# A short form for the last group of an expert, when it holds at most 128 rows

## The reference

```python
probs = softmax(x @ gate_w); w, sel = top_k(probs, 8); w = w / sum(w)     # 32 experts
# each expert takes its rows in order of token, at most C = 2048 of them
xg = x_pad[t_slot].reshape(E, C, H)
g = einsum('ech,ehi->eci', xg, w_gate)      # 512 -> 192
u = einsum('ech,ehi->eci', xg, w_up)        # 512 -> 192
y = einsum('eci,eih->ech', silu(g) * u, w_down).reshape(E * C, H)
out = zeros((T + 1, H)).at[t_slot].add(w_slot[:, None] * y)
```

## Time and profile before

| | |
|---|---|
| median of 3 runs | 2157.45 us (2155.42 to 2159.64) |
| span of the profiled execution | 2155.5 us |
| expert phase in it | about 1096 to 2145 us |
| PE busy | 1944.1 us, 90% |
| DVE busy | 1582.7 us, 73% |
| ACT busy | 1203.0 us, 56% |
| POOL busy | 1575.2 us, 73% |

### The profile page before, as it was taken

One profiled execution on the slowest core, in us unless ns is written; L12 is line 12 of the kernel. 1 busy time (PEld: TensorE's weight loads), 2 busy tenths in 40 slices (PEclk: granted clock), 3 DMA queues, 4 the chain that ended last, 5 costly groups with the idle time before them and its releaser, 6 DMA issues. The chain is left out here.

```text
span 2155.5 us, 66447 instructions
## 1 busy us (share of the span) xinstructions
PE 1944.1 (90%) x22263; PEld 1463.4 (68%) x22296; DVE 1582.7 (73%) x3230; ACT 1203.0 (56%) x3018; POOL 1575.2 (73%) x1776
## 2 busy tenths in 40 slices
PE   0799999999999999997259999999999999999997
PEld 0677667777667766675146777777777777777775
DVE  5688888888888888985236676777766667767664
ACT  3466666666666666665135555555554555545553
POOL 6336778777777777876667777777767777777775
PEclk9999999999999999999579999999999999999999
DMA  3111110111101111101048888777788888887876
GB/s 108 38 34 37 40 39 30 34 34 40 39 29 34 34 39 39 32 27 43 16 111 172 186 193 160 176 181 171 167 178 186 170 178 182 169 190 156 184 153 103
DMA packets 141452, 222.72 MB, mean 103 GB/s; under 512 B 32944, under 2 KB 65840, under 8 KB 141360
## 3 DMA queue, kind: packets, MB, share of 16 engines
q0 software_dynamic: 74752, 144.02, 33.9%
q1 hardware_dynamic: 62000, 69.24, 10.4%
q10 hardware_dynamic: 4608, 8.39, 1.0%
HBM read 136.34 MB, written 96.73 MB: 108 GB/s over the span
## 5 line engine op out<-in xcount | busy, mean ns | idle before, releaser
L2162 POOL DMA_INDIRECT out_dram<-y,m_add x300 | 498.1, 1660 | 171.0 <-POOLq L2170 112.5
L2288 PE MATMUL ps<-xh,wh 128*128 128x256 f16 x1752 | 398.3, 273 | 4.7 <-PEq L2300 4.7
L2289 PE MATMUL ps<-xh,wl 128*128 128x256 f16 x1752 | 398.3, 273 | 0.0
L2154 POOL DMA_INDIRECT xg<-z_scratch,slot_t x292 | 295.8, 1013 | 96.4 <-issue 83.4
L630 POOL DMA_INDIRECT slot_scratch<-pair,slots x256 | 304.8, 1191 | 70.2 <-issue 58.1
L2365 ACT ACTIVATE y<-ps,wts_now 128x512 f32<-128x512 f32 x294 | 185.2, 681 | 143.4 <-ACTq L2364 143.4
L2293 PE MATMUL ps<-xl,wh 128*128 128x256 f16 x1752 | 239.0, 273 | 1.3 <-PEq L2304 1.3
L2439 DVE SCALAR_TENSOR_TENSOR hx<-ps,s 64x256 f16<-64x256 f32 x146 | 62.2, 426 | 216.3 <-DVEq L2462 215.6
L2381 ACT ACTIVATE xh<-ps 128x512 f16<-128x512 f32 x146 | 87.2, 597 | 224.0 <-ACTq L2380 224.0
L2288 PEld LDWEIGHTS ps<-xh,wh 128*128 128x128 f16 x1752 | 171.3, 98 | 45.9 <-issue 12.8
L2289 PEld LDWEIGHTS ps<-xh,wl 128*128 128x128 f16 x1752 | 171.4, 98 | 33.1
(11 more groups left out here) (345 smaller groups left out, 5001.4 us busy)
## 6 DMA issues: line engine op xcount, KB each, us to landing
wst<-in_L_ffn_w_gate_dram SPq DMA_DIRECT2D x32, 384.0 KB
wst<-in_L_ffn_w_up_dram SPq DMA_DIRECT2D x32, 384.0 KB
xt<-in_x_dram SPq DMA_DIRECT2D x32, 256.0 KB
ct<-in_ctx_dram SPq DMA_DIRECT2D x32, 256.0 KB, 2.6
out_dram<-x SPq DMA_DIRECT2D x32, 256.0 KB, 2.1
z_scratch<-zn ACTq DMA_DIRECT2D x32, 256.0 KB, 2.0
wdst<-in_L_ffn_w_down_dram SPq DMA_DIRECT2D x32, 256.0 KB
out_dram<-y,m_add POOLq DMA_INDIRECT x300, 5.1
```

What stands on the lines that cost most here:

```text
L2154: pool.indirect_dma_start(out=xg[b][:, h, :], out_offset=None, in_=z_d[:, :], in_offset=bass.IndirectOffsetOnAxis(ap=rows(h), axis=0)).the ...
L2162: pool.indirect_dma_start(out=acc_d[:, :], out_offset=bass.IndirectOffsetOnAxis(ap=m_add[:, k, h:h + 1], axis=0), in_=y[:, k, h, :], in_of ...
L2288: pe.matmul(ps[:, dst, 0:GROUP], wh[:, j, k, c0:c0 + P], xh[:, k, :], start=(k == 0), stop=False)
L2289: pe.matmul(ps[:, dst, 0:GROUP], wl[:, j, k, c0:c0 + P], xh[:, k, :], start=False, stop=False)
```

## The change

A last group of an expert with at most 128 rows gets a form of its own on PE, if it is group 2, 3 or 4. (`ends_short(n)` is true for 513 to 640, 769 to 896 and 1025 to 1152 rows.) Of the 32 experts 16 meet this: 0, 7, 9 and 10 with four groups and 2, 6, 11, 12, 18, 20, 23, 24, 25, 28, 29 and 30 with five.

In that form POOL gathers one half of 128 rows into a buffer `xs` of its own, after it has copied the 128 row numbers with an operation of its own; PE transposes 4 times instead of 8 and runs `gate_up` with 128 columns instead of 256. `down`, ACT and DVE do what they did, over all 256 columns (the second half holds old values, whose rows are not added to the output). The form stands once for each place of an expert in the program, behind groups 2 to 4 and the further ones. The further groups now all run in one small loop.

```diff
-            def written_out_groups(eng, n, group):
+            def written_out_groups(eng, n, group, least=1):
                 for g in range(2, USUAL):
-                    with eng.If(n > g * GROUP):
+                    with eng.If(n >= g * GROUP + least):
                         group(g, g)
                 with eng.If(n > USUAL * GROUP):
-                    group(USUAL, 2)
-                    with eng.Fori(USUAL + 1, NGRP) as g:
+                    with eng.Fori(USUAL, NGRP) as g:
                         with eng.If(n > g * GROUP):
-                            group(g, 3)
+                            group(g, 2)
+            def ends_short(n):
+                halves = (n - 1) // P
+                return (halves // 4) * ((16 - halves) // 8) * (1 - halves % 2) > 0
...
+                def gather_short(e, n):
+                    col = e * (CAP // P) + 2 * ((n - 1) // GROUP)
+                    pool.wait_ge(short_free, 1)
+                    pool.sem_inc(short_free, -1)
+                    pool.tensor_copy(short_rows[:, :], slot_t[:, bass.ds(col, 1), 0]).then_inc(short_rows_ready, 1)
+                    pool.wait_ge(short_rows_ready, 1)
+                    pool.sem_inc(short_rows_ready, -1)
+                    pool.indirect_dma_start(out=xs[:, :], out_offset=None, in_=z_d[:, :],
+                                            in_offset=bass.IndirectOffsetOnAxis(ap=short_rows[:, 0:1], axis=0)).then_inc(short_landed, 16)
...
-                    with pool.If(n > 2 * GROUP):
+                    with pool.If(n > 2 * GROUP + P):
                         gather_group(e, 2, 2)
                     add_rows(y_buffer(0))
-                    with pool.If(n > 3 * GROUP):
+                    with pool.If(n > 3 * GROUP + P):
                         gather_group(e, 3, 3)
+                    with pool.If(ends_short(n)):
+                        gather_short(e, n)
                     earlier_experts_added()
...
-                        with pool.If(n > 4 * GROUP):
+                        with pool.If(n > 4 * GROUP + P):
                             gather_group(e, 4, 4)
...
+                def turn_short():
+                    pe.reg_add(n_short, n_short, 16)
+                    pe.wait_ge(short_landed, pe.snap(n_short, min_val=16, max_val=16 * E))
+                    for bank, signal in ((0, rows_ps_act), (1, rows_ps_dve)):
+                        for n in range(2):
+                            k = 2 * bank + n
+                            m = pe.transpose(ps[:, bank, n * GROUP:n * GROUP + P], xs[:, k * P:(k + 1) * P], ident[:, :])
+                        m.then_inc(signal, 1)
...
-                            pe.matmul(ps[:, dst, 0:GROUP], wh[:, j, k, c0:c0 + P], xh[:, k, :], start=(k == 0), stop=False)
+                            pe.matmul(ps[:, dst, 0:cols], wh[:, j, k, c0:c0 + P], xh[:, k, 0:cols], start=(k == 0), stop=False)
...
                     group(1, 1)
                     n = count_of(pe, e)
-                    written_out_groups(pe, n, group)
+                    written_out_groups(pe, n, group, P + 1)
+                    with pe.If(ends_short(n)):
+                        turn_short()
+                        down(j, short_free)
+                        gate_up(j, P)
```

More of the change, by code:

```diff
@@ L2075, in build @@
             y = sb("y", [P, YBUF, 2, D])
+            xs = sb("xs", [P, D])
+            short_rows = sb("short_rows", [P, 1], U32)
+            short_landed = sem("short_landed")
+            short_free = sem("short_free")
+            short_rows_ready = sem("short_rows_ready")
             w_staged = sem("w_staged")
@@ L2208, in expert @@
                             gather_group(e + 1, 1, 1)
-                        with pool.If(n > 4 * GROUP):
+                        with pool.Else():
                             gather_group(e + 1, 0, 0)
@@ L2222, in expert @@
                         with pool.If(n > g * GROUP):
-                            gather_group(e, g, 3)
+                            gather_group(e, g, 2)
                             add_rows(y_buffer(g))
@@ L2227, in _ @@
                     pool.sem_inc(rows_free[b], 1)
+                pool.sem_inc(short_free, 1)
                 pool.wait_ge(slots_loaded, 16)
@@ L2249, in _ @@
                     pe.reg_mov(n_landed[b], 0)
+                n_short = pe.alloc_register("n_short")
+                pe.reg_mov(n_short, 0)
                 def turn(b):
@@ L2260, in turn, with down @@
                         m.then_inc(signal, 1)
-                def down(j, b=None):
+                def turn_short():
[6 more added lines that the diff above has]
+                        m.then_inc(signal, 1)
+                def down(j, free=None):
                     pe.wait_ge(hx2_ready, 2)
@@ L2268, in down @@
                         m = pe.matmul(o, hx2[:, t], dh[:, j, 1, :], start=True, stop=False)
-                        if h == 0 and b is not None:
-                            m.then_inc(rows_free[b], 1)
+                        if h == 0 and free is not None:
+                            m.then_inc(free, 1)
                         pe.matmul(o, hx2[:, t], dl[:, j, 1, :], start=False, stop=False)
@@ L2282, in down, with gate_up @@
                         pe.matmul(o, hl1[:, t], dh[:, j, 0, :], start=False, stop=True).then_inc(y_ps, 1)
-                def gate_up(j):
+                def gate_up(j, cols=GROUP):
                     def with_xh(c0, dst):
                         for k in range(KC):
-                            pe.matmul(ps[:, dst, 0:GROUP], wh[:, j, k, c0:c0 + P], xh[:, k, :], start=(k == 0), stop=False)
-                            pe.matmul(ps[:, dst, 0:GROUP], wl[:, j, k, c0:c0 + P], xh[:, k, :], start=False, stop=False)
+                            pe.matmul(ps[:, dst, 0:cols], wh[:, j, k, c0:c0 + P], xh[:, k, 0:cols], start=(k == 0), stop=False)
+                            pe.matmul(ps[:, dst, 0:cols], wl[:, j, k, c0:c0 + P], xh[:, k, 0:cols], start=False, stop=False)
                     def with_xl(c0, dst, signal):
                         for k in range(KC):
-                            m = pe.matmul(ps[:, dst, 0:GROUP], wh[:, j, k, c0:c0 + P], xl[:, k, :], start=False,
+                            m = pe.matmul(ps[:, dst, 0:cols], wh[:, j, k, c0:c0 + P], xl[:, k, 0:cols], start=False,
                                           stop=(k == KC - 1))
@@ L2311, in expert @@
                     turn(0)
-                    down(1 - j, 0)
+                    down(1 - j, rows_free[0])
                     pe.wait_ge(wh_ready[j], 1)
@@ L2318, in group @@
                         turn(b)
-                        down(j, b)
+                        down(j, rows_free[b])
                         gate_up(j)
```

## The result

The changed kernel takes 2153.09 us (median of 20 runs, 2148.77 to 2160.03), the kernel before 2157.82 us in the same series. The ratio is 0.9982, 95% interval 0.9975 to 0.9989: 4.7 us less, where 10.4 were forecast.

A forecast was written before the change was run, and what follows sets the result against it. PE was taken to bound usual groups in the expert phase. Short groups' 13.4 us less 2.5 (first passages) and 0.5 (loop entries) gave 10.4 us: span 2145.1, median 2147 us; range 2136 to 2156, the forecast's own 2142 to 2152.

The forecast's parts named there:

- What PE is spared: Short group on PE: four transposes fewer (0.44 us), 36 matmuls 0.056 us apart instead of 0.109 (1.91 us); 2.35 us each.
- What is late next: ACT/DVE chain after the first transpose (T) limits short groups' gain to 1.06 or 0.70 us; 13.4 us in all.
- rival C of the experiments: Set up after the measurement, for the shortfall: less of each part reaches the end than the margins say; no chance given.
- The tests on PE: Short-form test on PE, three register instructions and one branch: hidden behind queued matmuls, at no cost.
- The first passage through new code: PE stalls where the short form is first reached, three places, 0 to 2.7 us each; 2.5 us taken for all.
- Loop entries: Last group of three six-group experts needs one loop entry more: 0 to 0.9 us each, 0.5 us taken for all.
- POOL: One gather instead of two, plus a copy with a wait: 0.4 us taken for copy and wait together.
- Rival 1: PE alone counts: gain goes toward the whole 38 us, 2120 us, half way 2138 us; chance 9%.
- Rival 2: PE stalls 2.7 us fetching code at each of 16 short forms: net +30 us, 2187 us; chance 8%.
- Rival 3's second form: Gain eaten by first passages at their upper bound (8.1 us) with the loop's: 2153 to 2159 us; whole rival 12%.
- Rival 4: Granted clock falls for one group around each short group's change of expert: 2256 us; chance 1%.

The follow-up runs named there:

- dead: Changed kernel with the short form's code and tests in place but the test never true, so all groups run in full; 2161.38 us, ratio 1.0018.
- again: The changed kernel itself, repeated for its time and a second profile; 2154.16 us, ratio 0.9979 to the kernel before.
- oldloop: Changed kernel with the further groups written as before on all engines (one in line, the others in a loop); 2158.56 us, ratio 1.0007.
- no_tail_dve_old_2: Changed kernel without the short form in experts 30 and 31 and with DVE's further groups written as before; 2147.83 us, ratio 0.9949.
- gate_only: Changed kernel with only gate and up short (128 columns); both halves still gathered, eight transposes; 2156.04 us in one run.
- notail: Changed kernel with experts 30 and 31, written out behind the loop, without the short form; 2150.05 us, ratio 0.9961.

## Why the prediction was right in the loop and wrong in size

- *What PE is spared.* Right: 128-column matmuls 0.056 us apart, 1335.82 to 1336.65 for the first 16.
- *What is late next.* Right: `s2` at T+4.88 for T+4.80, DVE's last operation at T+7.69 for 7.59, gate and up at T+9.06 for 8.95. `down` starts at T+0.54 instead of T+0.44, which is the 0.1 us that all of these are late. The gain is 0.92 to 0.96 us where 1.06 stood, 0.60 to 0.64 where 0.70 stood, 0.76 for expert 29; rival C of the experiments holds for this 1.2 us. The waits of PE are 0.35 and 0.97 us for 0.56 and 0.65: their sum is near (1.32 for 1.21), their split isn't.
- *The tests on PE.* Right, 0.00 us at experts without a short group and with four or five groups, in the change and in dead.
- *The first passage through new code: the step that failed.* I gave it 2.5 us, with 0 and 8.1 as bounds, and counted only the short form's own code on PE, with at most 2.7 us for each place. The term measured about 7.2 us: -0.4 at the start and 7.6 in the tail, where the short group gives 1.0 back. Of the 7.6 us 4.3 hang on DVE, whose work the change doesn't touch, but whose text it shortened by a group (group 1 of expert 30 is 1.4 us shorter, group 2 is 1.2 longer, and the stall with the slow clock behind it costs 4.5). PE's own passages are 2.2: 0.65 ahead of the short transposes and 1.56 ahead of the last `down`. The last 1.1 lie behind POOL's last issue; their cause is open. In the second profile, again, the term is 12.4 us, over its bound. The bound for one stall was too low as well: DVE's is 3.47, PE's went to 2.88 in again and to 4.16 in oldloop.
- *Loop entries.* 1.0 us for the 0.5 taken, within the bounds; oldloop and no_tail_dve_old_2 bring it to 0 and 0.6.
- *POOL.* The copy takes 0.28 us and the wait behind it 0.82, more than the 0.4 taken, as the rows below show; nothing waited for it.

```profile
1316.73 0.28 POOL L2202 COPY short_rows<-slot_t 128x1 uint32 x1
1317.83 0.97 POOL L2205 DMA_INDIRECT xs<-z_scratch,short_rows  x1 [0.82 <-POOLq L2204]
```

- *The rivals.* Rival 1 didn't come: gate_only shows that the matmuls' saving mostly waits. Rival 2 didn't: in the loop from expert 2 on PE never stands ahead of the transposes of `xs`, though it does at experts 0 and 30, where they are passed for a first time (0.65 us once in the profiled execution, 1.93 and 2.88 in again). Rival 3's second form came: first passages near their upper bound, and a median of 2153.09 us at the lower edge of its range; only, most of them are DVE's. Rival 4 was placed wrongly: in the two groups around a short one of the loop the clock stays at 1.00, but it fell three times while the experts ran: at 1111.8 us behind a wait of 3.01, at 1135.7 behind two of 2.10 and 1.51, and in expert 30. Its argument that the clock stays up across waits of 2.7 us misread the page: in the trace of before it stayed up behind the wait at 1134.60 and fell behind the one at 1603.30, which the 40 slices hide.

Open: what an engine waits for in these stalls (no run shows it); why the clock fell behind some waits of 2 to 3 us and not behind others; the 1.1 us behind POOL's last issue, which come to between 0.7 and 1.6 us in every kernel with a short form in use, and not in dead; and why ACT stands on the slower chips.

## What to carry to other kernels

When work is taken from the busiest engine, step through the group once with the shorter times: the second chain decides, and here it let 0.95 of 2.35 us through. Written-out code that runs once is paid by its place in the program: an edit that leaves an engine's work alone but changes its text can move a stall of 3 us on it, so try such an edit with each engine's text as before, and keep a new form out of the code that runs once. Ask of a test on which engine it stands (here 0.00 us on PE, which has matmuls queued, and 0.6 to 1.3 us per expert on DVE). Before a difference is put down to the change, look at the granted clock at that place in both traces. A gain that ends on a tight chain may vanish on another chip; measure on more than one.

## What the runs showed of the hardware

- DVE stood up to 3.59 us (notail) in straight code with nothing to wait for, and the place moved with its own text alone: with the old text it stands 2.17 us ahead of `xl` in expert 30's group 1 (before; 2.03 in no_tail_dve_old_2), with the new one 3.47 ahead of `hh` of group 2 (the change). PE stood 4.16 us (oldloop) ahead of a form that it reached for the first time. The Trainium skill (Runtime: NRT & Kernel Launch, Instruction fetch mechanics) says that instructions come to an engine in blocks and that a taken branch out of the blocks at hand waits for a fetch. The traces have stalls that would fit that, at jumps on PE; that these are fetches no run shows. If DVE's in straight code is the crossing of a block, the page's remark that a crossing is mostly hidden doesn't hold for it here. No run shows a block's size.
- The granted clock fell to its lower level behind waits of PE of 2.54 us (the change, expert 30), 2.71 us (before, expert 16) and 2.15 us (notail, expert 16), and stayed at 1.00 behind waits of 2.83 us (the change, expert 16), 2.74 us (before, expert 1) and 3.04 us (oldloop, expert 16). The length of the wait alone doesn't decide it. A fall with PE at work cost some 1.7 us.
- DVE's arithmetic for a test takes 0.63 us of its queue (1.71 less 1.08 us), and the way to a form behind the usual groups, jumps and the new branch together, 0.74 (1.08 less 0.34).
- The same kernel took 2158 us on three chips and 2310 us on two. Of the difference of the profiled spans, 121 us lie in the attention phase (34.1 us instead of 29.7 for an iteration) and 33 in the loop over the experts, by waits of ACT and others that are longer there (in an iteration ACT's longest are 2.9 us instead of 1.7); in the attention phase the granted clock is lower too, 0.95 instead of 1.00 over that iteration.
